# A graph network layer on one core: one semaphore for every event instead of one for a chain of events, and ScalarE's second layer written out

## The reference, cut to what matters

```python
# x [6250, 256], 100000 edges (src, dst), sorted by dst
xn  = layernorm(x)
h   = relu(mean_over_edges(xn[src]) @ W1l.T + b1 + xn @ W1r.T)     # first layer
gnn = mean_over_edges(h[src]) @ W2l.T + b2 + h @ W2r.T             # second layer
mix = linear attention of xn over 8 heads, norm, MLP with gelu, norm
x   = x + gnn + mix
H   = gelu(layernorm(x) @ fW1 + fb1)                               # [6250, 1024]
p   = softmax(H @ fWg + fbg)                                       # 8 experts
x   = x + p[e] * (H @ fWd[e] + fbd[e])   with e = argmax(p)
```

## Time and profile before

| what | value |
|---|---|
| time, median of 3 (lowest to highest) | 2658.11 us (2653.17 to 2660.57) |
| the profiled execution's own time | 2660.92 us |
| its span, first to last instruction | 2659.1 us |
| mean granted TensorE clock | 0.875 of full speed |
| busy: PE, DVE, ACT, POOL | 2007.2, 1131.2, 554.4, 1662.2 us |
| chain that ended last: PE, "issue", POOL, DMA, DVE, DVEq | 44%, 10%, 9%, 6%, 4%, 2% of the span |

### The profile page before, as it was taken

The page is one execution under the profiler, slowest core; times in us unless marked ns, Lnnn a source line. Parts: engine busy times, 40 slices in busy tenths (PEclk is TensorE's granted clock), DMA queues, the critical chain, the costliest instruction groups (busy, mean ns, idle before and its releaser), DMA issues.

```text
span 2659.1 us, 53406 instructions
## 1 busy us (share of the span) xinstructions
PE 2007.2 (75%) x9589; PEld 1205.8 (45%) x9590; DVE 1131.2 (43%) x3223; ACT 554.4 (21%) x1269; POOL 1662.2 (63%) x1721
## 2 busy tenths in 40 slices
PE   3566778878788888884334567778888889959998
PEld 1244444545455555551011234334444445548886
DVE  5422223357667767763212223333434444362222
ACT  6423334422222222220000001111121222201110
POOL 2677777767767665637777777777766655114442
PEclk9988889989999999996555777899998999879999
DMA  5533444444434443423344344445444444225552
GB/s 176 163 113 116 116 117 121 122 118 128 127 115 130 115 120 106 117 73 99 103 119 122 113 133 130 145 131 156 138 153 135 138 130 142 73 81 166 164 166 73
DMA packets 154315, 332.55 MB, mean 125 GB/s; under 512 B 34181, under 2 KB 88423, under 8 KB 154245
## 3 DMA queue, kind: packets, MB, share of 16 engines
q0 software_dynamic: 85824, 248.21, 32.0%
q10 hardware_dynamic: 42630, 58.35, 6.3%
q1 hardware_dynamic: 25794, 25.32, 3.0%
HBM read 273.97 MB, written 58.72 MB: 125 GB/s over the span
## 4 chain that ended last, share of the span: by engine, by line
PE 44%; issue 10%; POOL 9%; DMA 6%; DVE 4%; DVEq 2%; ACT 1%; ACTq 1%; POOLq 1%; SPq 0%
PE bank L389 15%; PE bank L1203 10%; POOL G L505 9%; PE bank L1397 7%; DMA G<-hh_d,edges 4%; PE bank L1385 2%; PE bank L1338 2%; DMA mbuf<-qT_d 2%; PE bank L1209 2%; PE bank L1304 1%; PE bank L1225 1%; PE bank L1229 1%; PE bank L1283 1%; DVE S L639 1%; DVEq L366 1%
## 5 line engine op out<-in xcount | busy, mean ns | idle before, releaser
L505 POOL DMA_INDIRECT G<-hh_d,edges x782 | 755.4, 966 | 355.9 <-issue 224.4
L505 POOL DMA_INDIRECT G<-xh_d,edges x782 | 771.2, 986 | 316.3 <-issue 224.7
L1203 PE MATMUL bank<-G,S 128*128 x1960 | 625.8, 448 | 319.4 <-SPq L452 239.3
L639 DVE SCALAR_TENSOR_TENSOR S<-edges,tv,iota 128x512 f16<-128x512 f16 x490 | 343.8, 748 | 415.8 <-PE bank L1203 257.3
L1203 PEld LDWEIGHTS bank<-G,S 128*128 128x128 f16 x1960 | 210.7, 108 | 633.6 <-issue 497.8
L1201 PE MATMUL bank<-ones,S 128*128 128x1 f16 x980 | 168.6, 172 | 103.3 <-SPq L452 92.8
L389 PE MATMUL bank<-fw,x1T 128*128 128x512 f32 x392 | 197.8, 628 | 0.0
L1201 PEld LDWEIGHTS bank<-ones,S 128*128 128x128 f16 x980 | 96.4, 98 | 126.4 <-issue 112.0
L519 POOL DMA_INDIRECT out_dram<-G,node_s x56 | 57.0, 1018 | 147.4 <-DVE G L950 144.7
L646 DVE TENSOR_SCALAR lo<-bank,RC 128x256 f32<-128x256 f32 x98 | 47.4, 483 | 223.2 <-PE bank L1203 221.5
L514 POOL DMA_INDIRECT res<-hx_d,node_g x56 | 53.9, 963 | 112.7 <-DVEq L937 95.8
(11 more groups left out here) (216 smaller groups left out, 2924.9 us busy)
## 6 DMA issues: line engine op xcount, KB each, us to landing
hx_d<-mbuf ACTq DMA_DIRECT2D x49, 512.0 KB
G<-xh_d,edges POOLq DMA_INDIRECT x782
G<-hh_d,edges POOLq DMA_INDIRECT x782
big<-in_fwd_dram SPq DMA_DIRECT2D x8, 1024.0 KB, 5.9
qT_d<-abuf ACTq DMA_DIRECT2D x49, 128.0 KB
hh_d<-HL ACTq DMA_DIRECT2D x49, 128.0 KB
mbuf<-qT_d ACTq DMA_DIRECT2D x49, 128.0 KB
hx_d<-res ACTq DMA_DIRECT2D x49, 128.0 KB
```

Source lines behind the costliest of these rows:

```text
L505: e.indirect_dma_start(G[:, r, n % SC, :], None, table, bass.IndirectOffsetOnAxis(ap=srcx[:, n:n + 1], axis=0)).then_inc(d_g[r], 16)
L639: VI.done(e.scalar_tensor_tensor(S[:, u, :, :], dst[:, bass.ds(c * SC, SC)].unsqueeze(2).to_broadcast([P, SC, P]), tv[:, bass.ds(k, 1)], i ...
L1203: ins = e.matmul(AGG[:], S[:, u, j, :], G[:, bass.ds(slot, 1), j, :].rearrange("p a c -> p (a c)"), start=False, stop=False, skip_group_ch ...
```

## The change

It has four parts.

1. **One semaphore an event.** `Line` makes a semaphore for every event and raises each by a lead at the start (VectorE's list of `sem_inc`: 38 instead of 22). The leads are set so that nearly all waits of a finish, whatever tile of the pipeline they speak of, ask for the same value, t or t + 1. `Turn` holds these few registers, worked out once at the head of a finish or a turn; `t - back` changes a number in the program and no register, and a register for it is made only where it addresses memory (`raw`, `tile`).
2. **ScalarE's second layer** is no loop over turns of items any more, but 52 calls of `finish2` with t as a constant: no word, no `If`, no registers.
3. **Waits left out** in the register form of `finish1` and `finish2` on TensorE (two in `tr2`, one each in `hidden`, `hiddenT` and `logits`), on VectorE (`PX2` before L818), on ScalarE (`VMA` "q", once a turn) and on TensorE (`AMA` "v", once a turn), and the `hold`s of ScalarE's `finish2`.
4. **One wait more**: VectorE waits for "ag2" too at the head of `from_stats`.

```diff
 class Line:
-    def __init__(self, sem, names, credit=False):
...
+    def __init__(self, sem, name, events, lead=0, shared={}):
+        self.names, self.at, self.n = list(events), 0, len(events)
+        self.lead = {e: lead.get(e, 0) if isinstance(lead, dict) else lead for e in self.names}
+        self.given = {e: n for e, n in self.lead.items() if n}
...
+            self.sems[e], self.lead[e] = shared[e] if e in shared else (sem(f"{name}_{e}"), self.lead[e])
     def done(self, ins, name):
-        ins.then_inc(self.sem, 1)
+        ins.then_inc(self.sems[name], 1)
     def wait(self, eng, name, i, back=0):
-        eng.wait_ge(self.sem, i * self.n + (self.credit + self.names.index(name) + 1 - back * self.n))
+        n = self.lead[name] + 1 - back
+        if not isinstance(i, int):
+            eng.wait_ge(self.sems[name], i.plus(n) if isinstance(i, Turn) else i + n)
+        elif i + n > 0:
+            eng.wait_ge(self.sems[name], i + n)
+class Turn:
+    def __init__(self, eng, base, offsets, less=0, regs=None):
+        self.base, self.less = base, less
+        self.regs = regs or {o: eng.snap(base + o) if o else base for o in offsets}
+    def __add__(self, n):
+        return Turn(None, self.base, (), self.less - n, self.regs)
+    def plus(self, n):
+        n -= self.less
+        return self.regs[n] if n in self.regs else self.base + n
+def raw(i):
+    return i.base - i.less if isinstance(i, Turn) and i.less else i.base if isinstance(i, Turn) else i
...
-        PB1 = Line(sem("pe_hidden1"), ["tr2", "r2"])
+        PB1 = Line(sem, "pe_hidden1", ["tr2", "r2"], {"tr2": 2, "r2": 3})
...
-        AG2 = Line(sem("a_hid2"), ["g0", "g1"], credit=1)
+        AG2 = Line(sem, "a_hid2", ["g0", "g1"], 3)
...
         def part(e, t, back, do):
-                with e.If(t > back - 1):
-                    do(within(e, (t - back) & 63, TILES - 1 - back))
+                with e.If(t.base > back - 1):
+                    do(t - back)
+        def tile(e, t):
+            if isinstance(t, int) or not t.less:
+                return raw(t)
+            return within(e, raw(t) & 63, TILES - 1 - t.less)
...
@@ vector
-            for l in (VB1, AH1, VR1, AR1, VL2, PX2, PL2, PQ2, AG2, AH2, AMA, VMA, PMA, PAC, PMB, AS2, VD, VO, VT, AT, PY):
-                e.sem_inc(l.sem, l.credit)
+            for l in (PI, AM1, VB1, AH1, VR1, AX1, AR1, PT1, PH1, PB1, AM2, VX2, VL2, PO2, PL2, AT2, AG2, AH2, AMA, VMA, PAC,
+                      PMB, AS2, AMB, VO, VT, AT, PY):
+                for n, lead in l.given.items():
+                    e.sem_inc(l.sems[n], lead)
@@ vector, finish1 (and so in finish2, with the offsets 0, 1 and TILES + 2)
+                t = t if isinstance(t, int) else Turn(e, t, (0, 1))
                 part(e, t, 0, mean_of)
@@ vector, from_stats
+                after("ag2")
                 after("ag1")
                 rstds(e, VD, i, "", 2)
@@ vector, pass B
             with e.Fori(2, TILES - 1) as i:
+                i = Turn(e, i, (0, 1, 2))
                 front(i + 1, True, from_stats(i, True, True, lambda: read_items(i + 1)))
@@ vector, finish2
-                    PX2.wait(e, "tr", t, 1)
                     VX2.done(e.tensor_scalar(m_t[:], res_tile(t), lnt[:, 0:1], lnt[:, 6:7], ALU.subtract, ALU.mult), "xf")
@@ scalar, second layer
-            with e.Fori(0, TILES) as i:
-                for k, t, c, last in body_items(e, i, 2, ITEMS_2, 0):
-                    with e.If(last == 1):
-                        finish2(t)
-            for t in range(TILES, TILES + 3):
+            for t in range(TILES + 3):
                 finish2(t)
@@ tensor, finish1
                 def tr2(t):
-                    AR1.wait(e, "relu", t)
-                    AH1.wait(e, "hT", t, 1)
+                    if isinstance(t, int):
+                        AR1.wait(e, "relu", t)
+                        AH1.wait(e, "hT", t, 1)
...
+                t = t if isinstance(t, int) else Turn(e, t, (0, 1, 2))
                 part(e, t, 1, out1)
-                part(e, t, 2, tr2)
-                part(e, t, 2, r2)
+                part(e, t, 2, lambda t: (tr2(t), r2(t)))
                 part(e, t, 0, tr1)
@@ tensor, finish2 (and so AH2 in hiddenT, VL2 in logits)
-                        AG2.wait(e, f"g{b}", t, 1)
+                        if isinstance(t, int):
+                            AG2.wait(e, f"g{b}", t, 1)
...
+                t = t if isinstance(t, int) else Turn(e, t, (0, 1))
                 part(e, t, 2, trx)
                 part(e, t, 3, hiddenT)
```

More of the change, by code:

```diff
@@ L77, in skip, with __init__, done, wait @@
         self.at += 1
-        eng.sem_inc(self.sem, 1)
+        eng.sem_inc(self.sems[name], 1)
     def wait(self, eng, name, i, back=0):
-        eng.wait_ge(self.sem, i * self.n + (self.credit + self.names.index(name) + 1 - back * self.n))
+        n = self.lead[name] + 1 - back
[3 more added lines that the diff above has]
+            eng.wait_ge(self.sems[name], i + n)
+class Loop:
+    def __init__(self, sem, events):
+        self.sem, self.names, self.at, self.n = sem, list(events), 0, len(events)
+    def done(self, ins, name):
+        assert self.names[self.at % self.n] == name
+        self.at += 1
+        ins.then_inc(self.sem, 1)
+    def wait(self, eng, name, i, back=0):
+        eng.wait_ge(self.sem, i * self.n + (self.names.index(name) + 1 - back * self.n))
 def turns(eng, n):
@@ L316, in build @@
-        v_rt = Line(sem("v_rt"), [f"s{i}" for i in range(200)])
+        VI = Line(sem, "v_item", ["S"])
+        PI = Line(sem, "pe_item", ["sum"], NS)
+        s_sum = PI.sems["sum"]
+        VM1 = Line(sem, "v_mean1", ["cnt", "rc", "lo", "mean"])
+        AM1 = Line(sem, "a_meanT1", ["mT"], 1)
+        VB1 = Line(sem, "v_hidden1", ["hi", "hlo"], 2)
+        AH1 = Line(sem, "a_hiddenT1", ["hT"], 2)
+        VR1 = Line(sem, "v_res1", ["res"], 4)
+        AX1 = Line(sem, "a_xT1", ["xT"], 1)
+        AR1 = Line(sem, "a_relu1", ["relu"], 2)
@@ new lines, in build @@
+        PL2 = Line(sem, "pe_lg2", ["lg"], 3)
+        AT2 = Line(sem, "a_x2T", ["xT"], 2)
+        AG2 = Line(sem, "a_hid2", ["g0", "g1"], 3)
+        AH2 = Line(sem, "a_hidT2", ["e0", "e1"], 3)
+        AXA = Line(sem, "a_xTA", ["xT"])
+        AMA = Line(sem, "a_mixa", ["ek", "rk", "v", "eq", "rq"], {"v": 1})
+        VMA = Line(sem, "v_mixa", ["one", "k", "q"], {"k": 1})
+        PMA = Line(sem, "pe_mixa", ["kv", "q"])
+        PAC = Line(sem, "pe_acc", ["acc"], 1)
+        v_kv = Chain(sem("v_kv"), [f"s{i}" for i in range(20)])
@@ L317, in build @@
+        v_rt = Chain(sem("v_rt"), [f"s{i}" for i in range(200)])
         pe_rt, a_rt, s_et = sem("pe_rt"), sem("a_rt"), sem("s_et")
-        VP = Line(sem("v_perm"), [x + h for h in "01" for x in ("row", "tile", "node", "prob")])
-        PP = Line(sem("pe_perm"), ["sum0", "sum1"])
+        VP = Loop(sem("v_perm"), [x + h for h in "01" for x in ("row", "tile", "node", "prob")])
+        PP = Loop(sem("pe_perm"), ["sum0", "sum1"])
         s_perm, s_fbd = sem("s_perm"), sem("s_fbd")
@@ L821, in logits @@
                     PL2.wait(e, "lg", t)
-                    VL2.done(e.tensor_copy(LG[:, bass.ds(t, 1), :].rearrange("p a e -> p (a e)"), B6[:, 0:NE]), "lg")
+                    VL2.done(e.tensor_copy(LG[:, bass.ds(tile(e, t), 1), :].rearrange("p a e -> p (a e)"), B6[:, 0:NE]), "lg")
+                t = t if isinstance(t, int) else Turn(e, t, (0, 1, TILES + 2))
                 part(e, t, 0, mean_of)
@@ L1045, in _ @@
             xT_copy(AXA, xTm, 0)
-            with e.Fori(0, TILES) as i:
+            with e.Fori(0, TILES) as n:
+                i = Turn(e, n, (0, 1))
                 PMA.wait(e, "kv", i)
@@ L1261, in accumulate @@
                 PAC.done(ins, "acc")
-            for first, i in turns(e, TILES):
+            for first, n in turns(e, TILES):
+                i = n if first else Turn(e, n, (0, 1))
                 if not first:
                     accumulate(i - 1)
-                AMA.wait(e, "v", i, 1)
                 AXA.wait(e, "xT", i)
@@ L1272, in _ @@
                 PMA.done(ins, "q")
[L1273 removed]
+                items_of(body_items(e, n, 0, ITEMS_A, 0), range(ITEMS_A), 0, finish1)
             accumulate(TILES - 1)
```

170 lines of the change are left out of this document (79 added, 91 removed).

## The result

| | before | changed |
|---|---|---|
| time, median (lowest to highest) | 2655.64 us (2648.92 to 2660.57, 4 runs) | 2626.74 us (2623.0 to 2629.08, 4 runs) |
| the profiled execution's span | 2659.1 us | 2627.3 us |
| mean granted TensorE clock | 0.875 | 0.874 |
| PE busy | 2007.2 us | 1991.4 us |
| instructions in the trace, all kinds | 53406 | 47147 |

The ratio is 0.9892, 95% interval 0.9865 to 0.9918: 29 us faster. The forecast was 8 us, and its range went down to 2636 us.

A forecast was written before the change was run, and what follows sets the result against it. GpSimd's gathers bound some stages; elsewhere only its waits for TensorE could shrink. Terms -3.8 - 2.5 - 2.3 - 2.1 + 1.5 + 1.5 = -7.7 us, from the median 2658.1 to 2650.4 us; range 2636 to 2663.

The forecast's parts named there:

- The reading by stages: Time can be won only where GpSimd waits for TensorE: 70.4 us in pass B, 79.9 late in layer 2.
- `trx`: First in TensorE's finish2, late second layer: four fifths of the issue gap before L1209 go, -3.8 us.
- `hiddenT`: TensorE's L1338 behind trx, late second layer: its issue gaps go, -2.5 us.
- `out1`: TensorE's L1225, first in finish1, pass B: 70% of its 3.3 us gap goes, -2.3 us.
- ScalarE's layer: ScalarE's second layer written out: mT comes earlier, but no TensorE wait names it, 0 us.
- (a): TensorE's small gaps are refilled by waits for S or x1T; -0.6 us, 2657.5; chance 0.25.
- (b): Larger gain: sequencers late in more places; -22 us in layer 2, -4 in pass B, about 2632; chance 0.20.
- (c): Slower: VectorE's turn start in pass B costs in full, +9.8, setup +1.5, TensorE's gains refilled; 2669; chance 0.10.
- two costs of VectorE: Pass B turn starts with the ag2 wait and two registers, a quarter let through, +1.5 us; setup +1.5 us.
- `qT` load: ScalarE's turn in pass B: saved register steps bring the load TensorE waits for earlier, -2.1 us.
- Setup: VectorE's 16 more sem_inc at the start take 1.3 to 2.1 us; +1.5 us, passed on whole.
- the early second layer: Early in layer 2 GpSimd's gathers are the bound, so TensorE's savings there bring 0 us.

The follow-up runs named there:

- b_unroll: The kernel before with one edit, ScalarE's second layer written out; ratio to the kernel before 1.0005.
- x_l1: The changed kernel with TensorE's first-layer registers not shared and the two waits of tr2 put back; ratio to the kernel before 0.9935.
- x_pe: The changed kernel with TensorE's registers not shared and left-out waits put back, except AMA "v"; multiplications stay away; ratio to the kernel before 0.9974.
- x_act: The changed kernel with ScalarE's first-layer loops without shared registers, its second layer still written out; ratio to the kernel before 0.9889.
- x_allb: The changed kernel, registers not shared on all three engines, TensorE's waits put back; ratio to the kernel before 0.998; as x_all on the slow-stepping chip 0.9769.
- again: The changed kernel itself, run again beside x_l1; ratio to the kernel before 0.9887.
- d_steps: The changed kernel with twelve register instructions more at the head of TensorE's finish2; ratio to the kernel before 1.0068.
- d_halfb: The changed kernel with six register instructions more at the head of TensorE's finish2; ratio to the kernel before 0.9935; as d_half on the slow-stepping chip 0.958.
- e_mergeb: The changed kernel with TensorE's finish2 under one If; ratio to the kernel before 0.987; as e_merge on the slow-stepping chip 0.95.
- x_l2: The changed kernel with TensorE's finish2 registers not shared and its left-out waits put back, on the slow-stepping chip; ratio to the kernel before 0.9666.

## Why the prediction was wrong

**What held.** The reading by stages held: pass B and the late second layer gain, pass A and the setup don't, GpSimd's waits for TensorE shrink by 15.4 and 8.4 us. Three terms were nearly right: `trx` -3.8 forecast, 4.9 to 1.1 measured; `hiddenT` -2.5, measured 2.5 to 0.0; `out1` -2.3, measured -3.3. ScalarE's layer at nothing held.

**Rivals.** (a) falls: the waits that it names did not take up what the gaps lost. The one for `x1T` is 35.9 us in both; the one for `S` fell by 2.7 us and the one for gathered chunks grew by 3.1, so that the idle time before these products is 75.5 us in both. (b) had the right size, 2632, but in part by luck. It put 22 us on the second layer and 4 on pass B; undoing TensorE's part costs 11 us in the second layer and 13 in the first. Of the engines that it names only TensorE's sequencer is shown to matter. (c) falls: `Turn` and the ag2 wait added 0.4 us to VectorE's idle time at L339 in all of pass B, where the forecast took 5.9 and (c) 9.8, and undoing VectorE's shared registers (x_dve) changes nothing.

**The step that failed is the sum.** It added up four gaps of TensorE (-10.7 us) and two costs of VectorE (+3.0), and took the time in which TensorE is busy as given, without a reason. In the two profiles TensorE's gaps shrank by 16.0 us, neither cost came through, and TensorE was busy 15.8 us less, for which there was no term.

Of the gaps it is the `qT` load that was mis-sized: -2.1 us forecast, 6.6 measured. The term counted ScalarE's saved steps only. In pass B the wait was 15.9 us before and 14.6 in b_unroll; 9.3 and 7.4 in the two profiles of the changed kernel, 8.1 with TensorE's first layer undone (x_l1), 9.8 with x_pe, 10.3 with x_dve, 11.3 with x_act; and 15.4 only with all three engines undone (x_allb). So no one engine's registers carry it. That the order of ScalarE's and TensorE's turns to each other decides is a guess, and no run tries it.

The missing term, in pass B, goes with the clock. TensorE's mean clock there was 0.97 before. One such place in the kernel before, timeline of PE:

```profile
830.29 0.71 PE L1283 MATMUL bank<-mbuf 128*128 128x132 f32 x4 [1.26 <-DMA mbuf<-qT_d]
...
832.12 2.08 PE L389 MATMUL bank<-x1T,big 128*128 128x128 f32 x8 [0.90 <-ACT x1T L1087]
...
834.07 0.59 PE L1203 MATMUL bank<-G,S 128*128 x1
...
838.41 0.38 PE L1203 MATMUL bank<-G,S 128*128 x1
```

and the windows around it (length, busy, clock):

```profile
821.00:831.00 10.00, 8.02 (x42) 5.16 (x42) 7.09 (x23) 1.44 (x4) 7.73 (x8) 1.00 0.52 145
831.50:838.00 6.50, 5.88 (x26) 3.41 (x27) 4.32 (x19) 1.20 (x4) 2.65 (x3) 0.50 0.35 101
```

TensorE stood still for 1.26 us for `qT` and for 0.90 us for `x1T`; then the granted clock is 0.50 of full speed, where the window before has 1.00, and a one-hot product takes 0.59 us instead of 0.38 until it comes back. Pass B from the same gather to the same gather, kernel before, x_allb, changed kernel and again, a fence each:

```profile
690.00:1202.00 512.00, 434.89 (x2522) 277.74 (x2521) 360.58 (x1137) 120.33 (x334) 315.41 (x322) 0.97 0.39 111
```

```profile
696.00:1213.00 517.00, 439.68 (x2529) 281.57 (x2529) 362.55 (x1139) 119.82 (x334) 319.22 (x324) 0.95 0.39 111
```

```profile
688.00:1187.00 499.00, 428.56 (x2528) 275.22 (x2527) 357.23 (x1139) 117.16 (x334) 318.31 (x323) 0.98 0.40 115
```

```profile
688.00:1182.00 494.00, 425.52 (x2533) 273.61 (x2531) 357.22 (x1141) 117.36 (x334) 322.20 (x323) 0.99 0.39 116
```

Cut into slices of 1 us, the same stage shows how long the clock was at its low level, and in how many stretches (all in us):

| profile | `qT` wait | at low clock (stretches) | PE busy | length |
|---|---|---|---|---|
| before | 15.9 | 34 (7) | 435 | 513 |
| b_unroll | 14.6 | 31 (6) | 436 | 512 |
| x_allb | 15.4 | 48 (9) | 439 | 516 |
| x_pe | 9.8 | 21 (5) | 431 | 504 |
| changed | 9.3 | 17 (4) | 428 | 499 |
| x_act | 11.3 | 7 (2) | 427 | 499 |
| d_steps | 8.0 | 10 (3) | 427 | 497 |
| again | 7.4 | 7 (2) | 425 | 493 |
| x_l1 | 8.1 | 3 (1) | 426 | 498 |

All seven stretches of the kernel before begin between 0.7 and 2.2 us behind the end of a wait for `qT`, about where the wait of 0.90 us for `x1T` follows it. Six of its eight `qT` waits of 1 us or more have one behind them, and one of the nine shorter ones; the `x1T` wait, which stands in nearly every turn, has none without `qT`. In x_allb and x_pe one stretch each follows a wait for gathered chunks instead (1.3 and 1.8 us). Between the kernel before and the changed one pass B is 14 us shorter, one half of it gaps and the other half PE's busy time. Against again it is 19 us, 10 of them busy time, but again's profile is of one of its faster executions.

So the saved wait came back about twice. How far this is shown: from 48 us at low clock down to some 10 the busy time falls with it, and below that it stays at 425 to 427. The chip is not the cause, as x_allb shares its chip with d_halfb and e_mergeb (clock 0.99). But no run changed the wait alone. x_act and d_steps have about equal busy times with waits of 11.3 and 8.0 us; four waits of 1 us or more in x_l1 have no low stretch behind them; and x_pe and x_l1, with the same TensorE program in this stage, differ by 21 against 3 us at low clock. A single program's mean clock varies between 0.869 and 0.878 on its own; 0.007 of it go with some 10 us.

Late in the second layer the clocks are 0.92 and 0.93 in either kernel, and PE is busy 471 us before, 464 in the changed kernel, 463 in again, but 468 in b_unroll, whose TensorE program is the one before. So some 3 of these 7 us are the spread of single profiles, and for the rest I have no cause. Ends of matmuls are modelled, so that part of the gaps between short ones may be counted as busy.

**Smaller misses.** Setup: VectorE starts at 4.30 instead of 2.82 us, the +1.5 forecast, but the sum passed it on whole, and it is absorbed. Its wait for ScalarE before the first reciprocals, before and then changed, is what gives it back:

```profile
L587 DVE RECIPROCAL rstd<-sd 128x7 f32<-128x7 f32 x7 | 1.4, 202 | 13.4 <-ACT sd L982 13.4
```

```profile
L655 DVE RECIPROCAL rstd<-sd 128x7 f32<-128x7 f32 x7 | 1.4, 201 | 12.0 <-ACT sd L1053 12.0
```

And the early second layer was taken as bound by gathers alone; it is 3 us shorter here, and twelve more steps in finish2 lengthen it too (gathers 900 to 1190 take 388 us in d_steps and 377 in the changed kernel).

And the instructions that do nothing but wait: the forecast reckoned with one more a turn.
**What stays open.** TensorE's part accounts for 23 of 29 to 30 us. x_pe puts back 890 of the 1363. The last 6 us (x_pe 0.9974 and x_allb 0.998, both clear of 1) lie, as far as is known, in what no experiment put back: the products in the waits of all engines, `AMA` "v" on TensorE, and the waits left out on VectorE and ScalarE. In the first layer registers and waits seem to cost more together than apart, at the edge of the noise, and no profile shows where. The changed kernel without the ag2 wait was not tried: two of VectorE's steps would then meet in one buffer.

## What to carry to other kernels

Where an engine's loop is data-dependent, count the sequencer steps between the last queued instruction and the first one of the next block, on the engine that sets the pace. Here six steps more at that place cost 13 us of 2656 and twelve 48, by the gaps 0.09 us a step once the cover was used up; waits put back further down cost 2 us, within the noise. Steps on an engine that waits anyway, here VectorE and ScalarE, were worth nothing that could be told. And a sum of gaps can be too low where TensorE changes between two clock levels, here 1.00 and 0.50 of full speed: ask of each wait that goes whether the clock falls behind it.

## What the hardware showed that was not expected

On one chip the kernel before took 3452 us, at a mean granted clock of 0.77 (0.87 to 0.88 elsewhere). It left no profile there, but four of its relatives did. Chain of waits in e_merge there, pieces of VectorE's sequencer between one-hots:

```profile
1079.03 0.70 DVEq L707
1079.75 0.69 DVEq L707
1080.49 0.10 DVEq L707
...
1080.94 0.06 DVEq L707
```

The steps are not slow in general. A plain register operation takes 0.036 us in the median there, as it does elsewhere (0.036 to 0.038), but now and then one takes 0.70 and, more rarely, 1.4 us. Register operations and branches longer than 0.6 us, in the four profiles on that chip:

| | time of the execution | slow ones | of all |
|---|---|---|---|
| e_merge | 3251 us | 448 | 17495 |
| d_half | 3330 us | 544 | 18151 |
| x_l2 | 3326 us | 591 | 18371 |
| x_all | 3367 us | 662 | 19175 |

On the other chips none of them is longer than 0.43 us, in any profile. So on that chip some 3% of the steps stall, a kernel with more of them has more stalls, and the median times rise with the number of steps (3275, 3306, 3329, 3368 us). That is why the undone kernel x_all is still 2.3% faster than the kernel before there, and e_merge, with the fewest branches, 5.0%; this last step is an inference, as the kernel before was not profiled there. What makes the steps stall is not known.

Also not expected when the forecast was made: how dear steps at the head of a block become once they are exposed. Twelve register instructions in 49 finishes turned a gain of 1.1% into a loss of 0.7%.
